# Audio tower on one core: own distances in steps for each operation in the first and last three groups, late weights in five blocks, a new order within a step

## The reference

```python
h = patches(x) @ W.T + b                  # 46 patches of 16 samples a clip, 90*16 -> 192
n = layernorm(h)
s = (n @ Wq) @ (n @ Wk).T                 # causal mask, softmax
h = h + softmax(s) @ (n @ Wv)
y = layernorm(h)
p = softmax(y @ W_gate.T + b_gate)        # top 2 of 8 experts
qkv = y @ W_qkv.T + b_qkv + 2 * sum_e p_e * (y @ A_e.T) @ B_e.T
h = h + attention(q, k, v, 12 heads of 16) @ W_proj.T + b_proj
```

## Time and profile before

| | us |
|---|---|
| median of 3 runs | 655.1 |
| lowest and highest of them | 655.05, 660.72 |
| the profiled execution's own time | 658.63 |
| its span, first to last instruction | 656.9 |
| TensorE busy | 586.3 (89%) |
| VectorE busy | 483.5 (74%) |
| ScalarE busy | 355.6 (54%) |
| GpSimd busy | 381.8 (58%) |

### The profile page before, as it was taken

The page is one execution under the profiler, slowest core; times in us unless marked ns, Lnnn a source line. Parts: engine busy times, 40 slices in busy tenths (PEclk is TensorE's granted clock), DMA queues, the critical chain, the costliest instruction groups (busy, mean ns, idle before and its releaser), DMA issues.

```text
span 656.9 us, 20488 instructions
## 1 busy us (share of the span) xinstructions
PE 586.3 (89%) x7805; PEld 523.9 (80%) x7805; DVE 483.5 (74%) x1306; ACT 355.6 (54%) x688; POOL 381.8 (58%) x650
## 2 busy tenths in 40 slices
PE   3827798979999999999999999999999999887783
PEld 3726586869898989898989898989898897775673
DVE  5302457675888888888888888888887888986672
ACT  3434454655666666656666666565655545533331
POOL 6687646785767677676767676757575614121010
PEclk9977789998999999999999999999999999996876
DMA  8795622976494949594959595958584434461610
GB/s 201 162 181 124 152 66 63 164 183 102 124 159 136 160 133 162 136 168 137 155 147 168 139 159 143 161 144 154 150 153 90 77 69 70 72 95 30 106 35 19
DMA packets 75154, 82.94 MB, mean 126 GB/s; under 512 B 10137, under 2 KB 60645, under 8 KB 75057
## 3 DMA queue, kind: packets, MB, share of 16 engines
q1 hardware_dynamic: 75057, 81.63, 61.2%
HBM read 50.24 MB, written 13.57 MB: 97 GB/s over the span
## 4 chain that ended last, share of the span: by engine, by line
PE 74%; POOL 7%; DVE 6%; issue 6%; DMA 3%; ACT 2%; SPq 1%; POOLq 0%; ACTq 0%; DVEq 0%
PE ps_r L1324 23%; PE ps_tok L1316 6%; PE ps_tok L1317 6%; PE ps_tok L1318 6%; PE ps_p L1565 5%; POOL xs L641 4%; PE ps_s L1553 4%; PE ps_r L1316 4%; PE ps_r L1318 4%; PE ps_r L1317 4%; DMA raw<-x 3%; PE ps_r L1467 3%; PE ps_r L1595 2%; PE ps_r L1404 2%; PE ps_r L1480 2%
## 5 line engine op out<-in xcount | busy, mean ns | idle before, releaser
L641 POOL TENSOR_TENSOR xs<-raw,xs 90x368 f16<-90x368 f32 x192 | 163.9, 883 | 16.4 <-ACT xs L735 16.4
L1316 PE MATMUL ps_tok<-w_tok,xs 128*128 128x192 f16 x576 | 145.8, 253 | 2.9 <-issue 1.7
L1317 PE MATMUL ps_tok<-w_tok,xs 128*128 128x192 f16 x576 | 145.6, 253 | 0.0
L1318 PE MATMUL ps_tok<-w_tok,xs 128*128 128x192 f16 x576 | 145.4, 252 | 0.0
L649 POOL TENSOR_TENSOR ad<-ga,disp 128x384 f32<-128x384 f32 x16 | 13.4, 840 | 108.1 <-DVE disp L1151 108.1
L735 ACT ACTIVATE p2T<-ps_p 128x552 f16<-128x552 f32 x64 | 40.3, 630 | 65.7 <-PE ps_p L1565 53.8
L735 ACT ACTIVATE xs<-raw 90x736 f16<-90x736 f32 x96 | 75.5, 805 | 0.0
L1316 PEld LDWEIGHTS ps_tok<-w_tok,xs 128*128 128x128 f16 x576 | 66.8, 116 | 5.8 <-issue 1.9
L1317 PEld LDWEIGHTS ps_tok<-w_tok,xs 128*128 128x128 f16 x576 | 66.8, 116 | 1.7
L1318 PEld LDWEIGHTS ps_tok<-w_tok,xs 128*128 128x128 f16 x576 | 66.7, 116 | 0.3
L641 POOL TENSOR_TENSOR xe<-raw,xe 90x368 f16<-90x368 f32 x64 | 55.7, 883 | 17.8 <-ACT xe L735 17.8
(11 more groups left out here) (175 smaller groups left out, 1566.5 us busy)
## 6 DMA issues: line engine op xcount, KB each, us to landing
raw<-x SPq DMA_DIRECT2D x32, 1035.0 KB, 8.3
qk_scratch<-qk SPq DMA_DIRECT2D x32, 276.0 KB, 3.0
q<-qk_scratch SPq DMA_DIRECT2D x48, 138.0 KB, 7.1
k<-qk_scratch SPq DMA_DIRECT2D x48, 138.0 KB, 7.7
xs<-xe SPq DMA_DIRECT2D x30, 184.0 KB
v<-v2s SPq DMA_DIRECT2D x64, 73.3 KB
out<-h2b SPq DMA_DIRECT2D x16, 276.0 KB
xs<-xe SPq DMA_DIRECT2D x15, 149.5 KB
```

The costliest lines, as they stand in the source:

```text
L641: nc.gpsimd.tensor_tensor(lo, src, hi, ALU.subtract).then_inc(s_lo, 1)
L1316: mm(dst, stat[0], mov[0], start=start, stop=False)
L1317: mm(dst, stat[0], mov[1], start=False, stop=False)
L1318: return mm(dst, stat[1], mov[0], start=False, stop=stop)
```

## The change

LAG gets new distances, and a table MOVED of the same form gives for each operation how many steps earlier it comes in the first three groups and how many later in the last three. The middle groups keep LAG alone. STEPS is 32 in place of 24. Every distance is larger by about five, which leaves room ahead for the first groups. The function that tells the step:

```diff
+def step_of(op, n, g):
+
+    at = g + LAG[op][n]
+    if op in MOVED and g < 3:
+        return at - MOVED[op][n][g]
+    if op in MOVED and g >= GROUPS - 3:
+        return at + MOVED[op][n][g - GROUPS + 6]
+    return at
 ...
         def group(s, op, n=0):

-            g = s - LAG[op][n]
-            return g if 0 <= g < GROUPS else None
+            for g in range(GROUPS):
+                if step_of(op, n, g) == s:
+                    return g
+            return None
```

Two lines of the tables (the first number is the distance; in MOVED three numbers for groups 0 to 2, then three for 13 to 15):

```diff
-      "h2b": (5,), "ln2": (3,), "xn2": (3,), "xn2_twin": (3,), "xn_high": (2, 3), "x2_high": (3, 4),
+    "low": (4, 4, 4, 4, 4, 4, 4, 5, 5, 5, 5, 5, 5, 5, 5, 5), "ad": (8,), "ln1": (6, 6, 6), "h2b": (9,), "ln2": (7,),
+    "ad": ((0, 0, 0, 0, 1, 4),), "h2b": ((1, 1, 0, 1, 4, 4),), "ln2": ((0, 0, 0, 0, 0, 3),),
```

```diff
-        WEIGHTS_AFTER = {"pe": (("tok", 11), ("av", 1), ("ga", 0)),
-                         "act": (("xn_tile", 1), ("p1t", 0), ("ga_copy", 0)),
-                         "dve": (("stats1", 2), ("stats2", 0), ("logits", 0))}
-        WEIGHTS = (range(M_FROM, GA_FROM), range(GA_FROM, PR_FROM), range(PR_FROM, ALL))
+        WEIGHTS = [range(a, b) for a, b in ((M_FROM, GA_FROM), (GA_FROM, PR_FROM), (PR_FROM, PR_FROM + 4), (PR_FROM + 4, LORA_FROM),
+                                            (LORA_FROM, ALL))]
 ...
-                    if g is not None and g + 1 < GROUPS:
-                        sp.wait_ge(s_lo, g * 16 + (8, 16)[half])
-                        load_x(clips(g + 1, half), half)
-                        if g == 0:
-                            (middle_weights, late_weights)[half]()
+                    if g is not None and g > 0:
+                        sp.wait_ge(s_lo, g * 16 - (8, 0)[half])
+                        load_x(clips(g, half), half)
+                        if g == 1 and half == 1:
+                            middle_weights()
+
+                def late_weights():
+                    if group(s, "lateload") == 0:
```

More of the change, by code:

```diff
@@ L68 @@
-STEPS = 24
-RING_AT = {"g0": 1, "g1": 0, "pv3": 2, "at": 1, "ot0": 0, "sc": 2, "ot1": 1, "qk0": 0, "qk1": 2, "qk2": 1, "pt": 0,
-           "cv0": 2, "av0": 1, "av1": 0, "pr0": 1, "xt0": 0, "pv0": 0, "cv1": 2, "xt1": 0, "yt0": 1, "pr1": 2,
-           "yt1": 1, "pv1": 2, "ga": 1, "v0": 0, "v1": 2, "pv2": 0}
-HIGH_AFTER = (3, 4, 5, 6, 8)
+LAG = {"store": (12,), "place_v2": (10,), "lateload": (6,), "load_next": (5, 5), "extra_rows": (6,),
+    "qk_to_scratch": (9,), "h_to_pairs": (7,), "stack_qk": (9,),
+    "low": (4, 4, 4, 4, 4, 4, 4, 5, 5, 5, 5, 5, 5, 5, 5, 5), "ad": (8,), "ln1": (6, 6, 6), "h2b": (9,), "ln2": (7,),
+    "xn2": (7,), "xn2_twin": (7,), "exp2": (9, 9, 10, 10), "x2_high": (8, 8), "wact": (3, 3, 4, 6, 7),
+    "xn_high": (6, 7), "high": (4, 4, 4, 4, 5, 5, 5, 5), "p2t_high": (9, 9, 10, 10), "ga_copy": (8,),
+    "g_high": (7, 7), "v_copy": (7, 7), "router_exp": (8,), "ad_high": (8,), "qk_high": (8, 8, 8), "exp1": (7,),
+    "p1t": (7,), "o2_twin": (10,), "xn_tile": (6, 6, 6), "cv_high": (8, 8), "o_high": (10, 10), "xn_twin": (6,),
+    "p2t_low": (9, 9, 9, 10), "max1": (7,), "ad_low": (8,), "norm2": (9, 9, 9, 10), "stats1": (5, 6, 6),
+    "max2": (9, 9, 9, 9), "wdve": (3, 3, 3, 5, 6), "shift": (9, 9, 9, 9), "qk_low": (8, 8, 8), "h_tile": (5, 5, 6),
+    "h2": (7, 7), "cv_low": (8, 8), "stats2": (7,), "o_low": (10, 10), "fin": (10, 10), "xn_low": (6, 6),
+    "x2_low": (7, 7), "logits": (7,), "g_low": (6, 6), "ranks": (7,), "dispatch": (7,), "sc": (9,), "at": (10,),
+    "wpe": (4, 4, 5, 6, 7), "tok": (7, 7, 7, 7, 7, 7, 7, 7, 7, 7, 8, 8), "pv": (11, 11, 11, 12),
+    "s": (11, 11, 11, 11), "qk": (10, 10, 10), "pt": (9,), "cv": (10, 10), "av": (9, 9), "p": (11, 11, 11, 11),
+    "ot": (12, 12), "xt": (8, 8), "pr": (12, 12), "yt": (9, 9), "ga": (9,), "g": (8, 8), "v": (8, 8)}
@@ L422, in unit_bank @@
             return (ps_s, ps_p)[n // 2 % 2][0:rows, n % 2, 0:cols]
-        def weights_due(s, engine, n):
-            op, k = WEIGHTS_AFTER[engine][n]
-            return group(s, op, k) == 0
         block = ctx.enter_context(nc.Block())
@@ L478, in middle_weights @@
                     load(b_qk[:, t:t + 1], b_qkv[128 * t:128 * (t + 1)].rearrange("(p a) -> p a", a=1), s_w2)
-            def late_weights():
-                for a in range(6):
-                    load(st_b[:, NR * a:NR * (a + 1)].rearrange("p (n r) -> p n r", n=N_EXP),
-                         B_lora[:, DH * a:DH * (a + 1), :].rearrange("n p r -> p n r"), s_w3)
             def step(s):
@@ L726, in step @@
                 low(4)
+                low(5)
+                low(6)
             for s in range(STEPS):
@@ L779, in weights @@
                 def weights(n):
-                    if weights_due(s, "act", n):
+                    if group(s, "wact", n) == 0:
                         for unit in WEIGHTS[n]:
@@ L1280, in step @@
                 weights(1)
-                xn_low(0)
+                p2t(0)
+                o_low(0)
+                o_low(1)
+                h_tile(0)
+                cv_low(1)
                 max2(2)
-                cv_low(0)
                 shift(2)
@@ L1286, in step @@
                 fin(0)
-                h_tile(0)
-                stats1(0)
-                cv_low(1)
+                xn_low(0)
+                weights(2)
+                p2t(1)
+                fin(1)
                 max2(3)
                 x2_low(0)
-                p2t(1)
-                fin(1)
+                x2_low(1)
+                shift(3)
                 xn_low(1)
-                shift(3)
-                x2_low(1)
                 norm2(1)
@@ L1300, in step @@
                 logits()
-                weights(2)
+                g_low(0)
                 ranks()
+                dispatch()
+                g_low(1)
                 norm2(2)
-                dispatch()
+                stats1(0)
             for s in range(STEPS):
@@ L1627, in step @@
                 qk_(2)
-                p_(0)
                 pt()
+                weights(0)
+                s_(1)
                 cv(0)
```

196 lines of the change are left out of this document (109 added, 87 removed), and 20 rows, old and new, of tables (LAG, MOVED).

## The result

| | us |
|---|---|
| changed kernel, median of 20 executions | 670.12 (659.97 to 675.1) |
| kernel before, median of 20 beside them | 657.53 (652.14 to 663.96) |
| ratio after to before, 95% interval | 1.0121 (1.0091 to 1.0151) |
| profiled execution of the changed kernel, its span | 672.51, 670.8 |

The change makes the kernel slower, by 1.2%. The forecast was 640, its range 630 to 650: wrong in sign. The ratio is taken over the fast executions alone (those within 1.5% of the kernel's fastest), where the change costs some 8 us, and the profiled execution of the changed kernel, 672.51, is not one of them, so the 13.9 us between the two traces overstate the change.

What follows compares the result with a forecast made beforehand. TensorE bounds the middle, waits bound the two ends; -11.7 - 5.1 - 5.1 + 5.2 = -16.7 us, taken as -15 after 1.7 kept for unseen waits, from a median of 655.1 to 640, range 630 to 650.

Steps and rivals of the forecast that it cites:

- Part 5: Middle periods and drain: operands and banks free before TensorE comes; middle cost 0, bounds 0 and +12 us.
- part 3: Fill: h2b of groups 0 and 1 one step earlier removes TensorE waits before 144.71 and 146.93; -5.1 us.
- Rival (c): Middle: TensorE waits on VectorE's turns once per period; at 2 us a period, 664 us; chance 0.06.
- Part 1: Fill: weight blocks and patch steps fill TensorE's 16.37 us wait before group 0's first transposes; -11.7 us.
- Part 2: Fill: short TensorE waits in group 0's attention and router go; -5.1 us, bounds 0 and -7.
- Part 4: Fill: group 2's fifth patch step waits for h_tile behind VectorE's lora units and clearings; +5.2 us, bounds 0 and +8.
- rival (b): Clearings don't hold TensorE (-5.2 us) and the drain's idle shrinks by 3 us; 631 us, chance 0.13.
- The drain: From group 13's router product on: almost the same sequence as before; 0 us, bounds -6 and +4.

Runs made afterwards that it cites:

- e3: Changed kernel with both swaps in SyncE's step undone (place_v2 behind load_next(0), stack_qk ahead of h_to_pairs): span 645.1 us, ratio to before 0.9826.
- e12: Changed kernel with SyncE's load_next(0) and extra_rows ahead of place_v2, and stack_qk ahead of h_to_pairs: span 639.2 us, ratio to before 0.9786.
- e7: e3's kernel with VectorE's three clearings moved from behind the lora units to the end of the same step: span 648.9 us, ratio to before 0.9903.
- e8: e3's kernel with the last three groups keeping the distances of the middle: span 647.9 us, ratio to before 0.9861.

## Why the prediction was wrong

- **Part 5, the middle, is the step that failed.** It said "every operand and every bank of the ring is free before TensorE comes to it". I had walked TensorE, VectorE, ScalarE and GpSimd through a period, and taken the operands that come by DMA as there, since in the middle of the kernel before they were. SyncE's list was never walked, though the diff shows `place_v2` going ahead of `load_next(0)` in plain text. The bound of +12 for the middle was too low for the same reason: it priced an unknown wait at 1 us a period, without the clock behind it. Measured: +24.0, made of 18.1 us of waits for the extra rows and 10.1 of clock behind them, less the 4.2 us by which the ten periods of before were longer than 332.
- **What the trace of before could have told.** The placement's 7.62 us stood in SyncE's queue, with the x load 0.5 us behind the router product. Moved behind it, the load starts some 8 us after the router product; with the 8.3 us that a load took in the median it lands at 16.4, and the extra rows after it, while the new list brings TensorE to them at 18.7 (207.44 less 188.78; 21.2 before). That sum gives no loss by itself, since it has neither the slower issue (up to 10.4 us) nor the slower landing (12.0), but it shows the slack gone. And the trace had a wait for extra rows (see part 3).
- **Rival (c)** had the sign, a middle of +24 and 664 us, but another mechanism, VectorE. e3 excludes it: with VectorE's list untouched the loss goes. That the number came out is luck.
- **Part 1**, mis-sized by 3 us: the weight blocks did go into the hole (41.73 to 51.7), but at the 1.2 GHz level, behind the 4.28 us of idle. In 41 to 57 us the clock is 0.50 (15.27 of 16 us busy), so the first transposes came at 57.22 in place of 53 to 54. I had allowed for half clock in the patch steps and not in the blocks. Idle before those transposes: 16.37 became 4.28 and small ones, as forecast. The second x load, issued at 27.68 with the nine middle loads behind it and no longer ahead, was there at 38.5, after 10.8 us (11.00 before), so it gained only by going out sooner.
- **Part 2**, right: from the router product of group 0 (88.92) to the transposes of ad (95.50) are 6.6 us in place of 15.1; forecast 93 to 97.
- **Part 3**, half misread. The 1.43 us before 144.71 are VectorE's h and so h2b; the 1.70 us before 146.93 ("issue") are a wait of `tok(0)` for the extra rows, for ScalarE's copy waits for them up to the same moment:

```profile
146.86 0.82 ACT L735 ACTIVATE xe<-raw 90x736 f16<-90x736 f32 x1 [1.11 <-DMA xs<-xe]
```

  It is the wait that the change made common, already in the trace of before. The wait for h is gone, and 6.22 us for the extra rows came instead at 139.89. With SyncE's cyclic order as before (e3) 2.33 us of that are left; in e12 TensorE has no wait over 0.75 us from 119 to 243 us.
- **Part 4**, right: 5.36 against 5.2, near 81 as walked (h at 81.70). But e7 says that it was no price to be won back: rival (b) counted it as such, and was wrong in that.
- **The drain**: 0 forecast, bounds -6 and +4; measured -4.5, within them. Rival (b) had 3 us for the table of distances, which e8 does not bear out.
- **The sum of the rest.** With SyncE's cyclic order as before (e3) the fill gives 11.9 us (195.4 to 183.5) against the forecast's 16.7 for it, and the median is 9.8 below that of before (645.96 and 655.71) against its 15. Only e12, whose order of SyncE is neither the one nor the other, comes to 17.2 in the fill and 14.8 in the median. There the terms offset one another (part 1 gave less, the drain more, the middle took 3), so that agreement is luck in part. My chance of 0.07 for slower was the real error: four engines walked out of five is no ground for 0.82.

## What to carry to other kernels

When a list is written anew, walk the DMA-issuing engine as well: for each transfer note when it is issued relative to the product that needs it, how long the issues ahead of it hold the engine, and what slack it had before. An issue row of several us is a block of work in that engine's list; keep the loads that others wait for ahead of it, and mind what stands directly ahead of a transfer in its own queue: here the rows were issued on time and landed late, behind a load. Delays that are harmless one by one (load later, consumer sooner) can add up to a wait, and a wait on TensorE costs more than its length where the clock falls behind it.
